# Softmax sums in two steps with GpSimd adding two key tiles, and another order at the end of attention

## The reference

```python
h = state_space(x)                       # 8 x 256 x 512
h = concat([h, txt], axis=1)             # 8 x 384 x 512
a = layernorm(h)
q, k, v = a @ Wq.T, a @ Wk.T, a @ Wv.T   # 16 heads of 32; 4 key/value heads
p = softmax(rope(q) @ rope(k).T / sqrt(32))
h = h + concat_heads(p @ v) @ Wo.T
x2 = layernorm(h)
w, e = top_k(softmax(x2 @ gate_w.T), 6)  # 64 experts, 64 places each, per sequence set
y = routed_experts(x2, w, e)             # silu(x @ w_gate) * (x @ w_up) @ w_down
y += silu(x2 @ sw_gate) * (x2 @ sw_up) @ sw_down   # shared expert, 704 hidden
return h + y
```

## Time and profile before

| | |
|---|---|
| three runs | 1418.71, 1427.5, 1435.67 us; median 1427.5 |
| the profiled execution's own time | 1441.19 us |
| its span | 1439.4 us, 23,556 instructions |
| PE busy | 1247.1 us (87% of the span) |
| DVE, ACT, POOL busy | 747.1 (52%), 417.8 (29%), 503.2 (35%) |
| softmax sums and values (L931) | 83.3 and 81.7 us of PE, 768 matmuls each |

### The profile page before, as it was taken

One profiled execution on the slowest core, in us unless ns is written; L12 is line 12 of the kernel. 1 busy time (PEld: TensorE's weight loads), 2 busy tenths in 40 slices (PEclk: granted clock), 3 DMA queues, 4 the chain that ended last, 5 costly groups with the idle time before them and its releaser, 6 DMA issues. The chain is left out here.

```text
span 1439.4 us, 23556 instructions
## 1 busy us (share of the span) xinstructions
PE 1247.1 (87%) x9192; PEld 798.8 (55%) x9192; DVE 747.1 (52%) x1667; ACT 417.8 (29%) x693; POOL 503.2 (35%) x453
## 2 busy tenths in 40 slices
PE   6263778889999999999898789999999999989995
PEld 5253534445555554546455778666666666656662
DVE  7994457666677878686864532332322223222221
ACT  2220314344445444445354411111111111111110
POOL 0000101111114444443557673334444543444444
PEclk9698669999999999999999889999999999999997
DMA  3024142312525251615165263999999999998983
GB/s 115 0 62 101 39 89 42 86 42 64 129 63 134 53 144 43 155 35 136 46 198 181 97 195 53 290 309 295 303 336 341 299 337 343 282 299 284 331 271 40
DMA packets 144310, 239.82 MB, mean 167 GB/s; under 512 B 64569, under 2 KB 84681, under 8 KB 144201
## 3 DMA queue, kind: packets, MB, share of 16 engines
q1 hardware_dynamic: 120360, 214.10, 46.7%
q0 software_dynamic: 23840, 24.23, 9.4%
HBM read 175.59 MB, written 38.90 MB: 149 GB/s over the span
## 5 line engine op out<-in xcount | busy, mean ns | idle before, releaser
L2063 POOL DMA_INDIRECT out_rows<-mo_y,mo_scatter_half x128 | 182.9, 1429 | 239.8 <-DMA out_rows<-mo_y,mo_scatter_half 152.2
L1404 DVE TENSOR_REDUCE at_maxes<-at_ps 128x1 f32<-128x384 f32 x384 | 196.3, 553 | 59.5 <-PE at_ps L947 51.6
L1171 ACT ACTIVATE bulk<-at_ps 128x1152 f32<-128x1152 f32 x128 | 144.5, 1129 | 252.8 <-PE at_ps L912 251.5
L1682 POOL DMA_INDIRECT slot_table<-at_toki,at_si x144 | 145.5, 1011 | 119.9 <-DVE at_maxes L1404 87.0
L70 PE MATMUL mo_ps<-arena_view,arena_view 128*117 128x384 f32 (+1 forms) x864 | 168.8, 344 | 1.1 <-PEq L570 1.1
L70 PEld LDWEIGHTS mo_ps<-arena_view,arena_view 128*117 128x117 f32 (+1 forms) x864 | 146.5, 179 | 14.6 <-issue 14.5
L947 PE MATMUL at_ps<-late_view,late_view 128*128 128x384 bf16 x384 | 117.5, 352 | 28.9 <-DVE at_maxes L1404 16.7
L903 PE MATMUL at_ps<-arena_view,arena_view 128*128 128x512 f32 (+1 forms) x576 | 114.9, 351 | 3.6 <-ACT arena_view L1256 2.1
L903 PEld LDWEIGHTS at_ps<-arena_view,arena_view 128*128 128x128 f32 x576 | 90.6, 193 | 36.1 <-issue 22.3
L947 PEld LDWEIGHTS at_ps<-late_view,late_view 128*128 128x128 bf16 x384 | 31.0, 98 | 138.5 <-DVE at_maxes L1404 103.0
L912 PE MATMUL at_ps<-arena_view 97*128 97x384 f32 x384 | 96.4, 360 | 8.3 <-DMA arena_view<-at_mrow 5.1
(11 more groups left out here) (222 smaller groups left out, 1771.8 us busy)
## 6 DMA issues: line engine op xcount, KB each, us to landing
bulk<-in_L_ffn_w_gate SPq DMA_DIRECT2D x32, 704.0 KB
bulk<-in_L_ffn_w_up SPq DMA_DIRECT2D x32, 704.0 KB
late_view<-in_L_ffn_w_gate SPq DMA_DIRECT2D x32, 704.0 KB
late_view<-in_L_ffn_w_up SPq DMA_DIRECT2D x32, 704.0 KB
arena_view<-arena_view SPq DMA_DIRECT2D x96, 192.0 KB
late_view<-in_L_ffn_w_down SPq DMA_DIRECT2D x32, 512.0 KB
bulk<-in_L_ffn_w_down SPq DMA_DIRECT2D x32, 512.0 KB
out_rows<-at_hr SPq DMA_DIRECT2D x8, 768.0 KB
```

The lines of the kernel that those rows point to most:

```text
L1171: A.activation(PT[:, N % RING, :, :], ps[:, 0:NT, 0:SEQ], ACT.Exp, scale=float(HD) ** -0.5)\
L1404: V.tensor_reduce(maxes[:, half, s, h:h + 1], ps[:, raw_bank(a, u), 0:SEQ], AX.X, ALU.max, negate=True)\
L1682: G.indirect_dma_start(slot_table, bass.IndirectOffsetOnAxis(ap=si[:, e % 2, m:m + 1], axis=0), toki[:, e % 2, m // TOPK:m // TOPK + 1], N ...
L2063: G.indirect_dma_start(acc_halves, bass.IndirectOffsetOnAxis(ap=scatter_half[:, half, 2 * p + e:2 * p + e + 1], axis=0), y[:, p % 2, e, co ...
```

## The change

Two parts, in one program.

First, the softmax sums. For all groups but the last sequence's (G < 28, the constant `ADDED`) GpSimd adds the exponentials of key tiles 0 and 1 (`add_pair_of_tiles`, one operation of 128x384 per head, 16 per iteration in b = 0 to 6). PE's sum is then step 0 over key tile 2 and step 1 over the added pair, and the third sum step is gone: 28 steps of four matmuls. The results lie in regions that belong to something else for part of an iteration: for g = 0 in the one of q's lo parts (free once `stack` has copied the second half), for g = 1 and 2 in that of the turned inputs (free once all three projections are done), for g = 3 in that of the rotation (free once the heads are turned). So an add waits for those, and whoever writes the regions next waits for the sums. The semaphore of `stack` is split in two, and `scores` waits for both.

Second, the end of the attention block, after the last values: another order of the same work on PE, ACT, DVE and POOL, scatters of the last iteration spread over other slots, and the first of the three output products of a shared unit starts before the last chunk of its hidden layer is there.

```diff
@@ -71,9 +71,9 @@
...
         return m
-    def out_of_hidden(self, T, out, s):
+    def out_of_hidden(self, T, out, s, chunks=None):
         last = 3 * self.SC - 1
-        for n in range(last + 1):
+        for n in range(last + 1) if chunks is None else range(3 * chunks[0], 3 * chunks[1]):
             c, (xa, wa) = n // 3, ((0, 0), (0, 1), (1, 0))[n % 3]
@@ -714,15 +716,22 @@
...
         LAST_TURN_SLOT = {3: (0, 1), 4: (2, 3)}
-        LAST_SCATTERS = {6: (0, 3), 7: (3, 6), 8: (6, 9), 9: (9, 12), 12: (12, 15), 14: (15, 18)}
-        VALUE_STEPS = {0: (0, 1), 1: (2, 3), 2: (4,), 3: (5,)}
+        LAST_SCATTERS = {4: (0, 1), 6: (1, 4), 7: (4, 7), 8: (7, 10), 9: (10, 13), 10: (13, 15), 12: (15, 18)}
+        VALUE_STEPS = {0: (0, 1), 1: (2,), 2: (3,), 3: (4,)}
+        LAST_STEPS = {0: (0, 1), 1: (2, 3), 2: (4,), 3: (5,)}
+        ADDED = NKV * (B - 1)
+        def sum_steps(G):
+            return NT - 1 if G < ADDED else NT
         TURN_SLOT = {2: (0, 1), 3: (2, 3)}
...
+        PAIR_SUM = [part(arena, (15872, 6144, 7680, 10752)[g], [REP, SEQ]) for g in range(NKV)]
         def unit(u):
@@ -918,21 +928,28 @@
...
                 b, g = G // NKV, G % NKV
-                kt, sums = q % NT, 1 - q // NT
+                first = sum_steps(G)
+                kt, sums = (q, 1) if q < first else (q - first, 0)
+                if first < NT and sums:
+                    kt = NT - 1 - q
                 if q == 0:
...
                     wait(pe, max_ready, 0 if G else UNITS)
-                if q == NT:
+                if q == 1 and G < ADDED:
+                    pe.wait_ge(pair_added, REP * (G + 1))
+                if q == first:
                     pe.wait_ge(v_copied, NT * (b + 1))
...
                     w = ones[:, :] if sums else vv[:, b % 3, kt, HD * g:HD * (g + 1)]
-                    m = T.matmul(ps[HD * j:HD * (j + 1), 3 + sums, 0:SEQ], w, PT[:, (REP * G + j) % RING, kt, :],
-                                 start=(kt == 0), stop=(kt == NT - 1))
-                if q == NT - 1:
+                    added = q == 1 and G < ADDED
+                    probs = PAIR_SUM[g][:, j, :] if added else PT[:, (REP * G + j) % RING, kt, :]
+                    m = T.matmul(ps[HD * j:HD * (j + 1), 3 + sums, 0:SEQ], w, probs,
+                                 start=q in (0, first), stop=q in (first - 1, first + NT - 1))
+                if q == first - 1:
                     m.then_inc(sums_done, 1)
-                if q == 2 * NT - 1:
+                if q == first + NT - 1:
                     m.then_inc(pv_done, 1)
@@ -1061,11 +1078,16 @@
...
                 if s == 0:
-                    pe.wait_ge(s_hi_done, SC * (i + 1))
-                    pe.wait_ge(s_lo_done, SC * (i + 1))
+                    pe.wait_ge(s_hi_done, SC * (i + 1) - 1)
+                    pe.wait_ge(s_lo_done, SC * (i + 1) - 1)
                     pe.wait_ge(w_lo, PIECES)
...
                     wait(pe, so_ready, NT * i)
+                    shared.out_of_hidden(T, ps[:, out_bank(s), :], s, (0, SC - 1))
+                    pe.wait_ge(s_hi_done, SC * (i + 1))
+                    pe.wait_ge(s_lo_done, SC * (i + 1))
+                    shared.out_of_hidden(T, ps[:, out_bank(s), :], s, (SC - 1, SC)).then_inc(s_down_done, 1)
+                    return
                 if s == 2:
@@ -1131,23 +1154,23 @@
...
                 turn_x2(B - 2, k, (7, 6))
-            for i in range(4):
-                project_out(B - 1, i, 0)
             logits(B - 2)
-            for i in range(4, 12):
+            shared_unit(0)
+            for i in range(8):
                 project_out(B - 1, i, i // 4)
-            shared_unit(0)
             places(B - 2)
-            shared_unit(1)
-            shared_unit(2)
+            for i in range(8, 12):
+                project_out(B - 1, i, i // 4)
+            for u in range(1, 4):
+                shared_unit(u)
             turn_x2(B - 1, 0, (0, 1))
             turn_x2(B - 1, 1, (0, 1))
-            shared_unit(3)
+            shared_unit(4)
             turn_x2(B - 1, 2, (0, 1))
             turn_x2(B - 1, 3, (0, 1))
-            shared_unit(4)
+            shared_unit(5)
             logits(B - 1, 0)
-            for u in range(5, 9):
+            for u in range(6, 9):
                 shared_unit(u)
@@ -1304,23 +1328,27 @@
...
             logits_copied(B - 2)
+            for m in range(2 * KC, 2 * KC + 3):
+                weights_hi(m)
             gate_exponentials(B - 2)
-            for m in range(2 * KC, PIECES):
+            for m in range(2 * KC + 3, PIECES):
...
@@ -1591,28 +1623,27 @@
...
             divide(NKV * B - 1)
+            routing(B - 2, 4)
+            routing(B - 2, 5)
             residual(B - 1, 0, 0)
             row_statistics2(B - 1, 0)
-            routing(B - 2, 4)
+            routing(B - 2, 6)
+            for m in range(2 * KC, 2 * KC + 3):
+                weights_lo(m)
             residual(B - 1, 1, 1)
             row_statistics2(B - 1, 1)
-            routing(B - 2, 5)
+            routing(B - 2, 7)
+            for m in range(2 * KC + 3, PIECES):
+                weights_lo(m)
             residual(B - 1, 2, 2)
             statistics2(B - 1, NT - 1)
-            routing(B - 2, 6)
-            routing(B - 2, 7)
             mult_shared(0, 0)
+            slots(B - 2)
             lo_shared(0, 0)
-            slots(B - 2)
-            for m in range(2 * KC, 2 * KC + 3):
-                weights_lo(m)
-            mult_shared(0, 1)
-            lo_shared(0, 1)
-            for m in range(2 * KC + 3, PIECES):
-                weights_lo(m)
+            for c in range(1, 3):
+                mult_shared(0, c)
+                lo_shared(0, c)
             routing(B - 1, 4)
-            mult_shared(0, 2)
-            lo_shared(0, 2)
             routing(B - 1, 5)
@@ -1653,6 +1684,20 @@
...
                 G.tensor_tensor(r1[:, s], r1[:, s], r2[:, s % 2], ALU.add).then_inc(rope_add, 1)
+            def add_pair_of_tiles(b, n):
+                g, N = n // REP, NH * b + n
+                if n % REP == 0:
+                    if g == 0:
+                        pool.wait_ge(stacked[1], STACK * (b + 1))
+                    elif g in (1, 2):
+                        pool.wait_ge(q_ready, NT * (b + 2))
+                        pool.wait_ge(kv_ready, NT * (b + 2))
+                    else:
+                        pool.wait_ge(heads_turned, NTILE * (b + 2))
+                pool.wait_ge(probs_ready, N + 1)
+                G.tensor_tensor(PAIR_SUM[g][:, n % REP, :], PT[:, N % RING, 0, :], PT[:, N % RING, 1, :],
+                                ALU.add).then_inc(pair_added, 1)
             def out_lo(N):
@@ -1702,6 +1747,8 @@
...
                         rope_sum(a, KV_SLOT[n - 1])
+                    if main and n != 0 and b < B - 1:
+                        add_pair_of_tiles(b, n)
                     if nxt and a + 1 < B and n == 7:
@@ -1710,6 +1757,8 @@
...
                         inverse_deviation2(d)
+                    if main and n == 0 and b < B - 1:
+                        add_pair_of_tiles(b, n)
                     if prev3 and b < B - 1 and n >= RAW_FROM:
@@ -1725,10 +1774,10 @@
...
             out_lo(NKV * B - 1)
-            scatter(B - 3, SCATTERED_LAST, SCATTERED_FIRST)
+            scatter(B - 3, 0, SCATTERED_FIRST)
+            places(B - 2)
             inverse_deviation2(B - 1)
             scatter(B - 3, SCATTERED_FIRST, SCATTERS)
-            places(B - 2)
             scatter(B - 2, 0, SCATTERS // 2)
...
```

More of the change, by code:

```diff
@@ L1076, in _ @@
                 for n in range(NH):
-                    G, steps = NKV * b + n // REP - 1, VALUE_STEPS[n % REP]
+                    G = NKV * b + n // REP - 1
+                    steps = (VALUE_STEPS if G < ADDED else LAST_STEPS)[n % REP]
                     of, units = raw_units(b, n)
```

33 lines of the change are left out of this document (22 added, 11 removed).

## The result

Four runs of the changed kernel took 1476.66 to 1483.51 us, median 1479.8; four of the kernel before, beside them, had a median of 1427.6. The ratio is 1.0367, with a 95% interval of 1.0316 to 1.0418: 52 us slower, where I forecast 16.5 slower and no more than 1462. The direction and the place in attention were right, the size was not, and the end gave next to nothing of its 15 us.

A forecast was written before the change was run, and what follows sets the result against it. PE's strict order was taken to bound attention, with waits and a lower clock at the end. Attention +31.5 and end -15 gave +16.5 on the 1427.5 median: 1444 us, range 1410 to 1462 at about 8 in 10.

The forecast's parts named there:

- the surest term: Slot 4: GpSimd's fifth add waits for kv(2) ahead of places, so turn_heads starts 7.8 us later, 5.3 without collisions.
- iterations 3 to 6: Attention iterations with places: each 8.8 us longer, 6.8 from delays and 2 from the clock, +35 together.
- 0 to 2: First three attention iterations: -1.5 us each in 0 and 1, 0 in iteration 2.
- The step itself: PE's softmax sums: each step taken out saves 0.75 us, 3.0 an iteration, 21.0 over 28 steps.
- slot 4: PE's second sum step: 2.0 us wait for the GpSimd add, plus some 2.4 if mask and adds collide on ports.
- part 2, the end: After the last values: waits of 11.3 us go and 3.7 of withheld clock returns; -15, between -4 and -23.
- My clock term: At the end, a quarter of 15.6 us withheld clock returns, 3.7; in attention, new waits cost 2 us an iteration.
- iteration 7: Last attention iteration: keeps its sums except for one step of the sequence before, -0.5 us.
- the base: Whole kernel: the summed change of +16.5 us was put on the median of three runs, 1427.5.
- D: The end: logits copy's remote release does not move, only the first wait goes; end -4, total 1455 us; chance 0.13.
- Rival B: Attention waits are cheap, no collisions or clock lost, +13; end gives nearly all, -22; 1418 us; chance 0.25.
- rival C: Attention: up to 5.6 us idle behind turn_heads an iteration hides the delay, saved steps remain; 1398 us; chance 0.15.

The follow-up runs named there:

- the runs of the end alone: Kernel before with only the new end order: 1432.1 us, ratio 1.0021; also with down weights behind and inverse deviation ahead of places: 1433.6, ratio 1.0003.
- the last run: Changed kernel with first group's sums moved, later adds, mended end, and last iteration's scatters in old slots: 1413.2 us, ratio 0.9899 to the kernel before.
- the run before that one: Changed kernel with first group's sums moved, mended end, adds of slots 4 and 5 behind the last rope_sum: 1417.8 us, ratio 0.9931.

## Why the prediction was wrong

**Right: the place and mechanism in attention.** The wait before `turn_heads` behind the fifth add was called the surest term. It came where and as forecast, and undoing it alone took back 18 us. For iterations 3 to 6 I had +35.2, the profile shows +33.2; for 0 to 2, -3.0 against -1.1. That the sums agree so well is in part luck: in iteration 4 `turn_heads` came 8.8 later and the iteration was 8.2 longer, where I had 7.8 and 8.8. The step itself was priced rightly: 2.7 us an iteration without adds, 3.0 forecast.

**Right, though split otherwise: slot 4.** The two waits were 3.0 us together, not 4.4, but the lower clock behind them cost more: the projection took 4.61 us, before 3.01. I gave the clock 2 us an iteration for both waits; 1.6 went in that one row. The sum behind my figure was off as well: 15.6 us over six waits are 2.6 a wait, not some 2, and a quarter of 15.6 is 3.9, not 3.7.

**Wrong, the main failure: part 2, the end.** The prediction had "End: -15, between -4 [...] and -23"; it was -1.7, and nothing in the runs of the end alone. The failing sentence is that new waits at `turn_x2` of the last sequence "can take the place" of two of 3.64 and 2.60. The waits that I counted as gone did go; the new wait was 11.28 and took all of it back. I had ScalarE's move of `weights_hi` ahead of the gate exponentials in front of me, and gave no price to it: it was read as a reordering of work that is ready, but that work waits for a copy that landed only 25.4 us after the start of the last scores (798.09 to 823.47). In the kernel before, ScalarE came to the same work 27.4 us after the last scores (762.48), behind a logits copy that was itself late (787.78), and found the copy there:

```profile
789.87 3.21 ACT L1238 ACTIVATE arena_view<-arena_view 118x512 fp32r<-118x512 f32 x6
```

Now the logits are copied at 811.10, 13.0 us after the last scores, and what was gained there is lost in front of `weights_hi`. Moving the weights took 14 us from the end in the profile and 17 from the median. With the weights behind, the end takes 121.8 us in the mean of five profiles, against 132.1 in four with the old order: some 10 of the 15 were there to be had. My clock term can't be judged, since 6.8 to 15.4 us of clock were withheld in those four profiles of the same old end.

**Wrong: the last 15 slots.** I put iteration 7 at -0.5 and the table of its scatters at nothing, without naming what hides them. It was +5.3; the run with the old table took 7.5 us less there than the run beside it, and 4.6 less by the medians.

**Wrong: the base.** I put a difference read from one execution on the median of three runs. The profiled execution of before stood 13.7 above that median, that of after 3.0 below its own. Between the two profiles the change is +35.6, between the medians +52; against the 29 runs of before that were made in the end, 1431.0, it is +49. The difference of 13 to 17 us between the two ways can't be given to a stage from single profiles.

Together: the spans moved by 35.6 where I had 16.5. Of the 19 between, 13 are the end and 6 the last slots; the other terms nearly cancel (+1.9 in iterations 0 to 2, -2.0 in 3 to 6, -1.9 before attention, +1.7 in the experts). Of the rivals, D had nearly the right outcome for the end (-4), but not its mechanism: the event that it feared would stay, ScalarE's copy of the logits, moved from 25.3 to 13.0 us after the last scores. In the trace's semaphores that event is no remote one either: in the kernel before it is raised by PE's logits alone, at 787.76, 4.6 us after the 783.2 at which PE's timeline has them done. D's 1455 was still too low for the reasons above. Rival B is refuted by the collisions and the lower clock, rival C by iterations that grew by 8.2 us where `turn_heads` came 8.8 late: 0.6 was taken up, not 5.6.

## What to carry to other kernels

An instruction that is moved to an engine with time to spare must be costed by its place in that engine's order: list its own waits, and what stands behind it that another engine needs soon. The adds made the kernel 47 us slower in one order; the same adds, with the first group's sums in another place, stand in the last run, which is 18 us faster than the kernel before. The engine's load was not what cost: in the run before that one, with all 16 adds, iterations 3 to 6 are within 0.8 us of those without.

When an order is rewritten, look for every moved instruction that waits for a transfer, and take the time at which the transfer lands from the trace before giving it a place.

A range built on one profile needs the spread of the runs added to it, on both sides.

## What the hardware showed that I had not expected

Operations with a single tensor as input are stretched beside GpSimd too, not only those with two. VectorE's L1513, three multiplications of 128x64 by a scalar per row, took 2.86 us beside an add and a `rope_sum`, 0.72 in the kernel before (L1481), and 0.58 at 826.38 with GpSimd idle. In slot 5 of the run with the first group's sums elsewhere a cast (L1528) took 0.86 us beside an `out_lo`, and a scalar operation (L1530) 0.84 beside an add, in place of 0.18 and 0.17. VectorE and GpSimd in the changed kernel, then in that run:

```profile
519.30 2.86 DVE L1513 TENSOR_SCALAR late_view<-late_view,at_rsum 128x64 f32<-128x64 f32 x3
```
```profile
519.62 0.99 POOL L1698 TENSOR_TENSOR arena_view<-bulk 128x384 f32<-128x384 f32 x1
520.57 1.55 POOL L1685 TENSOR_TENSOR arena_view<-arena_view,arena_view 128x640 f32<-128x640 f32 x1
```
```profile
511.37 0.86 DVE L1528 CAST at_si<-at_sf 128x18 uint32<-128x18 f32 x1
...
512.34 0.84 DVE L1530 TENSOR_SCALAR at_tokf<-at_tokf 128x3 f32<-128x3 f32 x1
```
```profile
511.21 0.99 POOL L1702 TENSOR_TENSOR late_view<-arena_view,late_view 128x384 fp32r<-128x384 f32 x1
512.16 1.00 POOL L1697 TENSOR_TENSOR arena_view<-bulk 128x384 f32<-128x384 f32 x1
```

Each of the three VectorE rows ends within 0.1 us of the GpSimd operation beside it. The Trainium skill, SBUF — State Buffer, section SBUF: two separate sides, has the same lock for a VectorE operation in a two-port mode. The rows agree with it, though no row tells the mode of an operation.

In the changed kernel PE's two waits of slot 4, 1.12 and 1.91 us with 0.44 us of work between them, were followed by a granted clock of 0.50 at 522 to 524, with PE busy all that time; the one of 5.19 us by 0.50 until 542. The run with the fifth add behind `places` had the same two waits in iteration 4 and kept a clock of 1.00. So the waits alone do not decide it, and what does is not shown.
